# Attention row maxima by a predicated copy and one reduction for both heads, with new orders of calls on all engines

## The reference

```python
mod = (silu(c) @ w_mod).reshape(8, 6, 1, 256)
sa, ca, ga, sb, cb, gb = (mod[:, i] for i in range(6))
ga, gb = (sign(g) * maximum(abs(g), 0.25) for g in (ga, gb))

def attn(x):                       # 16 heads of 16 channels
    h = layer_norm(x) * ln1_w + ln1_b
    q, k, v = h @ Wq + bq, h @ Wk + bk, h @ Wv + bv
    scores = q k^T / 4, only where 0 <= i - j <= 128
    x = x + softmax(scores) @ v @ Wo + bo
    h2 = layer_norm(x) * ln2_w + ln2_b
    return x + gelu(h2 @ W1 + b1) @ W2 + b2          # 1024 hidden

def mix(x):                        # prev: x one position earlier
    r = sigmoid((mu_r * x + (1 - mu_r) * prev) @ W_r^T)
    k = square(relu((mu_k * x + (1 - mu_k) * prev) @ W_k^T))
    return r * (k @ W_v^T)

x = x + ga * attn(layer_norm(x) * (1 + ca) + sa)
x = x + gb * mix(layer_norm(x) * (1 + cb) + sb)
```

## Time and profile before

| | |
|---|---|
| median of three runs | 722.39 us (721.84 to 722.66) |
| the profiled execution | 721.3 us, of which the span (first to last instruction) is 719.5 us |
| PE busy | 610.8 us, 85% of the span |
| PEld busy | 502.3 us, 70% |
| DVE busy | 535.6 us, 74% |
| ACT busy | 470.0 us, 65% |
| POOL busy | 350.4 us, 49% |
| mean granted TensorE clock | 0.921 |
| chain that ended last | PE 51%, ACT 15%, DVE 15%, issue 10%, POOL 5% |
| DVE, fused instruction of maxima (L1015) | 512 instructions, 425 ns mean |
| DVE, read of its accumulator (L1015) | 512 instructions, 140 ns mean |

### The profile page before, as it was taken

One profiled execution on the slowest core, in us unless ns is written; L12 is line 12 of the kernel. 1 busy time (PEld: TensorE's weight loads), 2 busy tenths in 40 slices (PEclk: granted clock), 3 DMA queues, 4 the chain that ended last, 5 costly groups with the idle time before them and its releaser, 6 DMA issues.

```text
span 719.5 us, 15228 instructions
## 1 busy us (share of the span) xinstructions
PE 610.8 (85%) x5110; PEld 502.3 (70%) x5110; DVE 535.6 (74%) x1890; ACT 470.0 (65%) x808; POOL 350.4 (49%) x497
## 2 busy tenths in 40 slices
PE   6656676679798999899989999999999997999994
PEld 4333454447686788778877877787778786889873
DVE  7586798775888879896988798879887867443422
ACT  2414654658497868786888688867886776773431
POOL 4102525352727483639373846474746554663431
PEclk9866566659999999999999999999999998999998
DMA  3342432131214120332033302331313131100010
GB/s 118 119 150 58 103 98 47 35 93 45 61 35 115 45 74 23 89 93 70 17 87 101 82 17 72 103 91 26 80 40 78 39 81 40 37 21 25 31 36 29
DMA packets 56858, 46.86 MB, mean 65 GB/s; under 512 B 26235, under 2 KB 48061, under 8 KB 56782
## 3 DMA queue, kind: packets, MB, share of 16 engines
q1 hardware_dynamic: 54950, 45.04, 23.6%
q10 hardware_dynamic: 1832, 0.87, 0.4%
HBM read 18.11 MB, written 4.23 MB: 31 GB/s over the span
## 4 chain that ended last, share of the span: by engine, by line
PE 51%; ACT 15%; DVE 15%; issue 10%; POOL 5%; SPq 2%; DMA 2%; POOLq 0%; ACTq 0%; DVEq 0%
PE bank L391 13%; DVE bank L1015 7%; ACT p L690 6%; PE bank L439 3%; PE bank L299 3%; PE bank L427 3%; PE bank L376 3%; PE bank L267 3%; PE bank L322 2%; PE bank L349 2%; PE bank L378 2%; PE bank L377 2%; ACT L752 2%; ACT kt_hi L664 2%; PE bank L234 2%
## 5 line engine op out<-in xcount | busy, mean ns | idle before, releaser
L1015 DVE CUSTOM_DVE_ANT_0 bank<-bank,mask 128x256 f32<-128x256 f32 (+1 forms) x512 | 182.3, 425 | 55.9 <-PE bank L267 55.9
L690 ACT ACTIVATE p<-bank,scale_s 128x384 f32<-128x384 f32 (+1 forms) x256 | 121.0, 542 | 50.3 <-PE bank L299 49.3
L391 PE MATMUL bank<-w,hid 128*128 128x256 f32 x512 | 117.1, 382 | 0.0
L1433 POOL TENSOR_SCALAR_AFFINE_SELECT p<-p 128x448 f32<-128x448 f32 x64 | 40.2, 629 | 152.2 <-ACT p L690 151.9
L391 PEld LDWEIGHTS bank<-w,hid 128*128 128x128 f32 x512 | 94.9, 190 | 13.0 <-issue 1.4
L700 ACT ACTIVATE p_hi<-p 128x1344 f16<-128x1344 f32 x64 | 84.5, 1320 | 26.8 <-POOL p L1438 26.7
L1446 POOL TENSOR_TENSOR p_lo<-p,p_hi 128x1344 f16<-128x1344 f32 x32 | 87.8, 2745 | 17.7 <-ACT p_hi L700 17.7
L299 PE MATMUL bank<-q_st,k_st 100*128 100x192 f16 (+2 forms) x512 | 70.2, 251 | 25.8 <-DVE nmax L1015 11.1
L376 PE MATMUL bank<-bt_hi,w_hi 128*128 128x256 f32 x256 | 76.4, 298 | 2.0 <-ACT hid L752 2.0
L299 PEld LDWEIGHTS bank<-q_st,k_st 100*128 100x128 f16 x512 | 39.6, 102 | 50.5 <-DVE nmax L1015 16.7
L377 PE MATMUL bank<-bt_lo,w_hi 128*128 128x256 f32 x256 | 72.3, 282 | 0.0
(11 more groups left out here) (181 smaller groups left out, 1431.0 us busy)
## 6 DMA issues: line engine op xcount, KB each, us to landing
k_st<-kt_hi SPq DMA_DIRECT2D x128, 64.0 KB, 2.0
v_blk<-vn SPq DMA_DIRECT2D x64, 66.0 KB, 2.3
q_st<-qt_hi SPq DMA_DIRECT2D x128, 32.0 KB, 1.9
k_st<-kt_lo SPq DMA_DIRECT2D x64, 64.0 KB, 2.0
x<-x SPq DMA_DIRECT2D x16, 256.0 KB, 2.8
out<-x SPq DMA_DIRECT2D x16, 256.0 KB, 2.4
xa<-x SPq DMA_DIRECT2D x7, 512.0 KB, 5.3
q_st<-qt_lo SPq DMA_DIRECT2D x64, 32.0 KB, 1.9
```

The source lines that it names most:

```text
L391: last = e.matmul(dst, hid[:, m, t * P:(t + 1) * P], w2[:, m, :], start=(m == 0), stop=(m == MF - 1))
L690: e.activation(p32[gp % 2][:, i * 2 * QW:i * 2 * QW + w], ring_s.at["st", gp, i][:, 0:w], ACT.Exp, scale=scale_s[:, 1:2]).then_inc(s_ex, 1)
L1015: last = e.tensor_tensor_reduce(out=scores, in0=scores, in1=mask[:, 2 * P - w:2 * P], scale=1.0, scalar=NEG, op0=ALU.add, op1=ALU.max, acc ...
```

## The change

The diff has two parts. The first replaces VectorE's maxima. Before, for every bank and each of its two heads one fused instruction adds a mask (0, or -3e38 where a key is not allowed) and takes the maximum along the row. After, a predicated copy overwrites the own tile's columns above the diagonal, of both heads at once, with the columns of the tile in front (in the first query tile with column 0, which every query may see), and one tensor_reduce then takes both heads' maxima of the bank. Copies and reductions go by two banks: two copies, then two reductions, each of which waits for its copy's semaphore s_mov. The mask has a new form: `later`, ones above the diagonal and zeros elsewhere, 127 columns for two heads, made by one memset and one affine_select instead of one and two, so POOL_CONST is 7 instead of 8.

```diff
-                w = P if qt == 0 else 2 * P
+                own = 0 if qt == 0 else P
+                if u == 0 and qt == 0:
+                    e.wait_ge(s_pool, POOL_CONST - 1)
+                hold(e, s_mtt, u)
+                tile = lambda j: ring_s.at["mx", u, qt, j][:, :].rearrange("p (c a) -> p c a", a=2)
                 for j in range(first, last_):
                     e.wait_ge(s_mxm, 16 * u + HQ * qt + j + 1)
-                    if qt == 0 and j == 0:
-                        hold(e, s_mtt, u)
-                    for a in range(2):
-                        scores = ring_s.at["mx", u, qt, j][:, a:2 * w:2]
-                        last = e.tensor_tensor_reduce(out=scores, in0=scores, in1=mask[:, 2 * P - w:2 * P], scale=1.0, scalar=NEG,
-                                                      op0=ALU.add, op1=ALU.max, accum_out=nmax[:, a, j, qt:qt + 1])
-                    last.then_inc(s_mx, 1)
+                    allowed = tile(j)[:, 0:P - 1, :] if own else tile(j)[:, 0:1, :].broadcast_to([P, P - 1, 2])
+                    e.copy_predicated(tile(j)[:, own + 1:own + P, :], later[:, :, :].bitcast(I16), allowed).then_inc(s_mov, 1)
+                for j in range(first, last_):
+                    e.wait_ge(s_mov, 16 * u + HQ * qt + j + 1)
+                    e.tensor_reduce(nmax[:, :, j, qt], tile(j)[:, max(own - 1, 0):own + P, :].rearrange("p c a -> p a c"),
+                                    AX.X, ALU.max).then_inc(s_mx, 1)
```

The second part is the order of calls, rewritten on all five engines. The start on VectorE and SP, the first half of TensorE's loop, and the tail:

```diff
 # VectorE, start
             low_a(0)
             setup_wqk()
-            setup_exp()
+            low_qk(0)
             setup_wv()
-            setup_mod()
-            low_qk(0)
-            setup_rows()
             maxima(0, 0, 0, 2)
             maxima(0, 0, 2, 4)
+            setup_mod()
             maxima(0, 1, 0, 2)
+            setup_rows()
             maxima(0, 1, 2, 4)
...
 # VectorE, loop, first half
+                residual_a(u - 2)
+                stats_b(u - 2)
+                low_p(gp + 1)
+                maxima(u + 1, 1, 0, 2)
+                maxima(u + 1, 1, 2, 4)
+                low_p(gp + 2)
                 normalise(gp)
-                residual_a(u - 2)
-                maxima(u + 1, 1, 0, 2)
-                stats_b(u - 2)
-                maxima(u + 1, 1, 2, 4)
                 mix(u - 4)
-                low_p(gp + 1)
...
 # SyncE, start
             load_attn()
-            rows_mod()
             load_x(1)
             load_rest()
             rows_bias()
+            rows_mod()
             load_mod_a(1)
-            stacks(0)
...
 # TensorE, loop, first half
+                out_project(u - 2)
                 context(gp)
-                out_project(u - 2)
                 maxima(u + 1, 1)
...
 # TensorE, loop, odd half
-                values_b(u - 5)
                 max_rows(u)
                 project(u + 1)
+                values_b(u - 5)
+                if u == 1:
+                    setup_bias()
                 context(gp - 1)
...
 # TensorE, tail
+            transposes_d(NU - 2)
             down(NU - 1, 0)
-            transposes_d(NU - 2)
             down(NU - 1, 1)
+            keys(NU - 2)
             receptance(NU - 2)
-            keys(NU - 2)
             values_b(NU - 2)
             transposes_d(NU - 1)
+            keys(NU - 1)
             receptance(NU - 1)
-            keys(NU - 1)
             values_b(NU - 1)
...
 # ScalarE, tail
             modulate(NU - 1)
+            square(NU - 1)
             gate(NU - 1)
-            square(NU - 1)
```

More of the change, by code:

```diff
@@ L14 @@
 P = 128
-NEG = -3.0e38
 EPS = 1e-5
@@ L72, in adaln_block @@
         ident = sb("ident", [P, P])
-        mask = sb("mask", [P, 2 * P], BF16)
+        later = sb("later", [P, P - 1, 2], BF16)
         mhalf = sb("mhalf", [P, NT])
@@ L598, in _ @@
             up(NU - 3, 2, 3)
+            transposes_d(NU - 4)
             transposes_c(NU - 1)
@@ L601, in _ @@
             out_project(NU - 2)
-            transposes_d(NU - 4)
             down(NU - 3, 0)
+            out_project(NU - 1)
+            transposes_b(NU - 2)
             down(NU - 3, 1)
-            transposes_b(NU - 2)
-            out_project(NU - 1)
+            receptance(NU - 4)
             keys(NU - 4)
@@ L613, in _ @@
             values_b(NU - 4)
+            down(NU - 2, 0)
             transposes_d(NU - 3)
-            down(NU - 2, 0)
-            receptance(NU - 3)
             transposes_b(NU - 1)
             down(NU - 2, 1)
+            receptance(NU - 3)
             keys(NU - 3)
@@ L1271, in _ @@
             maxima(0, 3, 0, 2)
-            maxima(0, 3, 2, 4)
             for b in range(B):
                 u, gp = 2 * b, 8 * b
-                low_p(gp - 3)
-                normalise(gp - 2)
+                maxima(u, 3, 2, 4)
+                low_b(u - 3)
+                gated(u - 5)
                 low_p(gp - 2)
@@ L1304, in _ @@
                 low_b(u - 2)
-                low_m(u + 1)
-                normalise(gp + 2)
-                low_p(gp + 2)
-                low_p(gp + 3)
-                gated(u - 4)
+                add_y(u - 3)
                 if u == 0:
@@ L1315, in _ @@
                                                in1=w1_hi[:, k, :].bitcast(F32), op0=ALU.mult, op1=ALU.subtract).then_inc(s_w1l, 1)
+                low_m(u + 1)
+                low_p(gp + 3)
+                normalise(gp + 2)
                 low_qk(u + 2)
-                add_y(u - 3)
+                gated(u - 4)
+                stats_x(b + 2)
                 normalise(gp + 3)
                 maxima(u + 2, 0, 0, 2)
-                first_column(u - 3)
+                output(u - 4)
                 maxima(u + 2, 0, 2, 4)
-                stats_x(b + 2)
+                residual_b(u - 3)
@@ L1497, in setup_const @@
                 e.memset(ident[:, :], 0.0).then_inc(s_pool, 1)
-                e.memset(mask[:, :], 0.0).then_inc(s_pool, 1)
+                e.memset(later[:, :, :], 1.0).then_inc(s_pool, 1)
                 e.wait_ge(s_pool, 4)
@@ L1704, in _ @@
                 u, gp = 2 * b + 1, 8 * b + 4
-                stacks(u + 1)
-                store(u - 5)
-                load_residual(u - 3)
+                store(u - 6)
+                load_x(b + 2)
+                load_mod_a(b + 2)
+            load_v(B - 1, 1)
+            load_residual(NU - 5)
+            load_mod_o(B - 3)
             load_mod_g(B - 2)
+            store(NU - 6)
+            load_residual(NU - 4)
+            load_mod_o(B - 2)
             store(NU - 5)
-            load_mod_o(B - 2)
-            load_mod_g(B - 1)
             load_residual(NU - 3)
             store(NU - 4)
+            load_mod_g(B - 1)
             load_residual(NU - 2)
             store(NU - 3)
+            load_residual(NU - 1)
             load_mod_o(B - 1)
-            load_residual(NU - 1)
             store(NU - 2)
```

211 lines of the change are left out of this document (104 added, 107 removed).

## The result

The changed kernel takes 726.78 us in the median of 18 runs (723.80 to 730.35), the kernel before 722.43 us in 18 runs (716.57 to 725.48). The ratio is 1.0064, 95% interval 1.0042 to 1.0087: the change is slower by 0.6%. The forecast was 718.6 us. The profiled execution took 727.48 us, with a span of 725.4 us against 719.5.

The account below looks back on a forecast made before the run. TensorE was taken as the steady bound, VectorE as busiest up to 162 us; maxima 0, start +4.8, loop -6.6, tail -2.0 gave -3.8 on 721.3, 717.5, plus 1.1 to the timed median: 718.6 us, range 705 to 732.

Parts of the forecast that it names:

- second rival: Start's delay at the 24 stack transfers stays, steady waits only change places; 725.3 us (721 to 731), chance 0.28.
- The loop, -1.1 us per period: Steady loop, 162 to 588.7 us and beyond: reordered calls cover TensorE's waits, -1.1 us over 6 periods, -6.6 us.
- values_b: TensorE, odd half: moved behind max_rows and project, it covers p_lo's wait (-0.4 us) but max_rows waits longer (+0.5).
- the pairs of maxima: VectorE's maxima in pairs, ahead of normalise, halve TensorE's 0.6 us wait for row maxima: -0.3 us per period.
- the swap: TensorE: out_project(u-2) ahead of context(gp), which covers the wait of maxima's matmuls for residual_a: -0.88 us per period.
- The new maxima, 0: VectorE: copy 0.36 us plus reduction 0.33 us a bank, 22.1 us a batch against 22.3, hidden by slack: counted 0.
- The start, +4.8 us: Start: later setup_rows delays the stack transfers, taken as on the path, +5.4 us; setup_gates -0.6; net +4.8 us.
- the lower bound of 4.2: Start: smallest delay by setup_rows' move, +4.2 us, if bias_rows gains more than mod_rows costs; upper bound +9 us.
- The tail, -2.0 us: Last half batches: receptance beside the squares spares values_b's wait, -1.35 us; earlier mix ahead of add_y, -0.6 us.
- add_y: Tail: transposes_d(14) ahead of down(15) brings half batch 14's mix earlier, so it no longer delays add_y: -0.6 us.
- no wait for x of L1058: Sign in the steady period: the 0.9 us wait of maxima's matmuls for residual_a's addition is gone.
- the first stack at 47 to 48 us: Sign at the start: the first stack transfer goes out at 47 to 48 us and not 42.27.

Follow-up runs that it names:

- fc_reduce: Changed kernel with first_column's two-element tensor_copy exchanged for a one-element tensor_reduce in the same place; 715.70 us, 0.9906 of the kernel before.
- fc_moved: Changed kernel with first_column, still a copy, put back between the halves of the maxima before (qt 0); 715.29 us, 0.9904 of the kernel before.
- order_fr: Changed kernel's new orders with the old maxima, and first_column's copy as a reduction; 715.55 us, 0.9908 of the kernel before.
- later_late: fc_reduce with GpSimd's affine_select for the mask `later` put behind its memset of v_blk; 714.98 us, 0.9891 of the kernel before.
- rows_back: fc_reduce with setup_mod and setup_rows directly around low_qk(0) and rows_mod first on SyncE, as before; 712.87 us, 0.9866 of the kernel before.
- order_alone: Changed kernel's order of calls with the old add-and-max maxima, first_column still a copy; 723.46 us, 1.0008 of the kernel before.
- swap_back: fc_reduce with TensorE's out_project(u-2) again behind context(gp) in the first half of a batch; 1.0037 of the kernel before.
- tail_back: fc_reduce with receptance again ahead of keys and gate ahead of square in the last two half batches; 0.9921 of the kernel before.
- op_alone: Kernel before with only the new maxima and their mask, old orders, first_column still a copy; 725.52 us, 1.0025 of the kernel before.

## Why the prediction was wrong

The forecast was 718.6 us, faster; the result is slower. Its second rival had the right side and nearly the size (725.3 us), by another mechanism than it named.

- **The loop, -1.1 us per period: this is the step that failed.** It priced out_project, values_b and the pairs of maxima, and did not price the other calls that moved. One of them was first_column, moved on VectorE from between the halves of one query tile's maxima to between those of the next. Counted at nothing, like the rest, it came to stand beside GpSimd's p_lo and cost 2.1 us per period: 75.34 with it, 73.2 without (fc_reduce and fc_moved). That this copy was put at nothing had no reason given: what GpSimd runs beside VectorE does not occur in the forecast's sum. Without it the loop gives -0.92 us per period against the forecast's -1.1, and the kernel 715.7 us.
- That 715.7 us is close to 718.6 us is luck. The -0.92 us contain the new maxima, which the forecast counted at 0 and which give 0.3 to 0.6 us of it; the start of fc_reduce is 0.6 us shorter than before's (225.41 for 225.98) and not 4.8 us longer.
- Of the loop's terms, the swap is right (0.84 for 0.88 us). values_b was taken at -0.4 + 0.5 = +0.1 us and is 0.0, but neither of its halves is right: the wait at max_rows is 1.1 us, and what values_b covers is a wait for csum and one for the row maxima, not p_lo. The -0.3 us for the pairs of maxima no run tries alone.
- **The new maxima, 0.** 0.33 us for the copy, not 0.36, 21.1 us a batch. Nothing in the total, but by two effects: less in the loop, and more in the start, which the forecast did not price. The four narrow banks (2.65 us in fc_reduce, 1.95 in order_fr) are 0.7 us of it. The mask's affine_select of 1.25 us ahead of the memset (rows above) delays the first transposes, but later_late shows nothing of that at the second batch. The larger part stays unexplained.
- **The start, +4.8 us.** Wrong in both parts. setup_rows moved by 4.1 us (35.73 to 39.83) and the first stack by 2.3 (42.27 to 44.56), below the lower bound of 4.2: bias_rows landed in 1.1 us and not in 2 to 2.5, and kt_lo was 1.5 us earlier, by moves ahead of it that were not priced. Nor does a later first stack delay the kernel by as much, as the forecast took for granted: rows_back's stacks start 3.9 us before fc_reduce's and the fourth batch no earlier. And the new orders as a whole make the start 3.0 to 5.3 us shorter (order_alone and order_fr against before: 222.96 and 220.72 for 225.98), not longer. The swap is one of the moves that do it (3.1 us, swap_back); the others were not tried. The granted clock up to 162 us is 0.64 after and 0.69 before; what this is worth was not parted from the rest.
- **The tail, -2.0 us.** The mechanism is right, the size 1.5 for 2.0. The last receptance runs beside the squares and values_b follows without a wait:

```profile
712.56 3.78 PE L427 MATMUL bank<-mixed,wb 128*128 128x256 f32 x8 [3.94 <-DVE mixed L1115]
716.13 2.17 PE L415 MATMUL bank<-wb,mixed 128*128 128x256 f32 x8
718.14 1.89 PE L439 MATMUL bank<-wb,mixed 128*128 128x256 f32 x8
```

The swap is 1.2 us (tail_back) for the forecast's 1.35. add_y starts 0.04 us behind down's end and not 0.35: 0.3 for 0.6. Of the signs that the forecast named, these came: 0.33 us from start to start, VectorE's busy time of a batch (64.64 us), no wait for x of L1058, values_b without a wait. These did not: the first stack at 47 to 48 us, and the period of 73.0 us.

The copy's hold could have been read from the kernel before: its trace has the tensor_scalar on sct lasting 1.30 us for 16 elements and ending with the memset of v_blk (6.03 and 6.01 us), and the copy at 391.17 us ending with GpSimd's operation (rows above).

```profile
4.73 1.30 DVE L1218 TENSOR_SCALAR sct<-sct 128x16 f32<-128x16 f32 x1
```

```profile
2.39 3.62 POOL L1508 MEMSET v_blk<- 128x4224 f16 x1
```

## What to carry to other kernels

When calls are put in a new order, look at every small VectorE copy or tensor_scalar from SBUF to SBUF that moved, and at what GpSimd runs where it now stands: its length is what is left of GpSimd's operation, and it changes when anything ahead of it gets shorter. What that costs depends on what waits behind it: 2.1 us of a period for a copy of 2.7 us, nothing for one of 0.45 us. A tensor_reduce over one element does the same copy and was not held. A change that is worth nothing in itself can still push such a copy into a hold (op_alone), so price all moved calls, or test the orders and the operation apart.

## What the runs showed of the hardware

- A two-element tensor_copy from SBUF to SBUF on VectorE lasted until GpSimd's current tensor_tensor ended, to within 0.03 us, in five kernels (0.29, 0.45, 1.18, 2.17, 2.71 us), and took 0.16 us where GpSimd was idle; a tensor_reduce with the same operands started inside GpSimd's operation and took 0.15 us; a tensor_scalar of 16 elements lasted until a GpSimd memset ended, in three kernels. The Trainium skill has this ("SBUF — State Buffer", section "Who interferes with whom"): VectorE and GpSimd share a pair of SBUF ports as an exclusive lock for the whole instruction, copies and tensor_scalar in their faster modes need it, and tensor_reduce never does on trn2. The times above agree with all three; the ports themselves, and the mode in which the copy ran, no trace shows.
- copy_predicated of 254 fp32 elements in PSUM with a 16-bit mask in SBUF: 0.33 us from start to start, as the reduction of 258.
- The 2 KB transfer bias_rows landed in 1.14 us when it was issued 14 us behind the weight loads, and in 5.17 and 5.3 us when it was issued 5 us behind them.
- An affine_select over 127 x 2 bf16 elements whose pattern has a stride of 0 took 1.25 us on GpSimd, one over 128 with one dimension 0.29 us.
